# Graph network kernel: the rows of h and y turned by DMA transposes instead of TensorE transposes

## The reference

```python
def _layer(x, rows, cols, vals, W, b):            # first network, layers 0 and 1
    neigh = segment_sum(vals[:, None] * x[cols], rows)   # mean over neighbours
    return relu(concatenate([x, neigh], axis=1) @ W.T + b)
h = _layer(x, src, dst, 1/deg, W0, b0); h = _layer(h, ..., W1, b1)
y = layernorm(x + h)
z = y @ W_self + segment_sum(top32(y @ W_neigh)[src], dst) / deg_dst
out = layernorm(y + z)
```

## Time and profile before

| | |
|---|---|
| time, 3 runs | 677.92 us median (676.73 to 679.54) |
| span of the profiled execution | 680.0 us |
| TensorE busy | 650.4 us (96% of the span) |
| VectorE busy | 496.9 us (73%) |
| ScalarE busy | 338.8 us (50%) |
| GpSimd busy | 108.6 us (16%) |
| DMA queue of SyncE | 72.30 MB, 35.8% of 16 engines' time |

### The profile page before, as it was taken

The page is one execution under the profiler, slowest core; times in us unless marked ns, Lnnn a source line. Parts: engine busy times, 40 slices in busy tenths (PEclk is TensorE's granted clock), DMA queues, the critical chain, the costliest instruction groups (busy, mean ns, idle before and its releaser), DMA issues.

```text
span 680.0 us, 11272 instructions
## 1 busy us (share of the span) xinstructions
PE 650.4 (96%) x3982; PEld 337.4 (50%) x3983; DVE 496.9 (73%) x1274; ACT 338.8 (50%) x654; POOL 108.6 (16%) x187
## 2 busy tenths in 40 slices
PE   8788899999988999999999999999999999999996
PEld 3466566676534444444444444444444444444442
DVE  8898969999768788787882587878878855643333
ACT  3768779999768576767673233333333320000000
POOL 3001122222111001010110323222232210000000
PEclk9898979999999899999999999999999999999999
DMA  8643635555521111111112556565656423310000
GB/s 205 116 130 108 214 120 167 171 167 167 158 67 46 31 37 40 33 44 31 46 32 69 158 159 186 153 190 152 180 163 178 137 80 115 116 31 24 25 28 23
DMA packets 39543, 73.09 MB, mean 107 GB/s; under 512 B 3120, under 2 KB 32207, under 8 KB 39481
## 3 DMA queue, kind: packets, MB, share of 16 engines
q1 hardware_dynamic: 39481, 72.30, 35.8%
HBM read 38.91 MB, written 33.38 MB: 106 GB/s over the span
## 4 chain that ended last, share of the span: by engine, by line
PE 81%; DVE 10%; ACT 3%; DMA 2%; issue 2%; SPq 0%; POOL 0%; DVEq 0%; POOLq 0%; ACTq 0%
PE pair L1557 34%; PE bank L1681 10%; PE pair L1681 10%; PE bank L1481 6%; PE bank L1455 5%; PE bank L1447 4%; PE pair L1455 4%; PE pair L1367 4%; DVE hots L637 2%; PE bank L1461 1%; DVE tree L820 1%; DMA own_in<-own_dram 1%; DMA wparts_dram<-w_parts 1%; PE pair L1346 1%; PE bank L1467 1%
## 5 line engine op out<-in xcount | busy, mean ns | idle before, releaser
L1557 PE MATMUL pair<-xs,ct 125*128 125x512 f16 x625 | 143.7, 380 | 0.0
L1557 PE MATMUL pair<-a,ct 125*128 125x512 f16 x625 | 142.8, 379 | 0.0
L637 DVE TENSOR_TENSOR hots<-iota,jobs 125x1792 f16<-125x1792 f16 (+1 forms) x100 | 103.1, 1064 | 5.0 <-PE pair L1367 4.4
L1557 PEld LDWEIGHTS pair<-a,ct 125*128 125x128 f16 x625 | 61.1, 99 | 68.1
L1557 PEld LDWEIGHTS pair<-xs,ct 125*128 125x128 f16 x625 | 60.9, 100 | 67.6 <-issue 1.4
L1068 ACT ACTIVATE slab<-pair 125x875 f16<-125x875 f32 (+1 forms) x100 | 83.3, 854 | 13.2 <-PE pair L1367 8.6
L1226 ACT ACTIVATE a<-ct 125x1000 f16<-125x1000 f16 (+1 forms) x75 | 80.2, 1069 | 8.2 <-DMA c_dram<-slab 7.3
L1681 PE MATMUL bank<-xs,ct 125*128 125x512 f16 (+1 forms) x325 | 71.5, 379 | 0.0
L1681 PE MATMUL pair<-xs,ct 125*128 125x512 f16 x300 | 66.4, 379 | 0.0
L529 POOL TENSOR_TENSOR own_in<-own_in,bias_sb 125x256 f32<-125x256 f32 x50 | 38.2, 765 | 168.3 <-DMA own_in<-own_dram 168.2
L1301 ACT ACTIVATE sd<-mv,epsb 125x1 f32<-125x1 f32 x25 | 7.4, 294 | 113.9 <-DVE mv L1004 113.9
(11 more groups left out here) (205 smaller groups left out, 829.7 us busy)
## 6 DMA issues: line engine op xcount, KB each, us to landing
c_dram<-slab SPq DMA_DIRECT2D x25, 683.6 KB
ct<-c_dram SPq DMA_DIRECT2D x25, 683.6 KB
own_in<-own_dram SPq DMA_DIRECT2D x50, 125.0 KB
own_dram<-own SPq DMA_DIRECT2D x25, 125.0 KB
own_dram<-own_st SPq DMA_DIRECT2D x25, 125.0 KB
x_in<-in_x_dram SPq DMA_DIRECT2D x25, 125.0 KB
z_dram<-z_st SPq DMA_DIRECT2D x25, 125.0 KB
a<-z_dram SPq DMA_DIRECT2D x5, 625.0 KB
```

The costliest lines, as they stand in the source:

```text
L637: v.tensor_tensor(hots[k][:, :, :, :].rearrange("p w g (a d) -> p (w g) a d", d=2), iota, job, ALU.is_equal).then_inc(win_hot, 1)
L1557: ins = mm(agg[k % 3][0:lhs.shape[1], :], lhs, parts[l][:, t, :], start=t == 0, stop=t == NT - 1, skip_group_check=True)
```

## The change

The 50 turns leave TensorE, and the 50 copies from PSUM leave ScalarE. In their place SyncE issues 50 DMA transposes (`turn(i)`), which read `part` (now 128 partitions high, its last rows cleared by GpSimd) and write `tr_sb` at once, four 128 x 128 blocks each. `turn` waits for the complete `part` and for the product that last read this `tr_sb`; `product` and the next writer of `part` wait for the semaphore that the DMA raises at its end (`turned`). In layer 1, `load_c(T - 1)` moves to the place right behind `turn`, ahead of `load_own`, `load_x` and `store_z`. A few products of the first tiles stand at other blocks.

```diff
-        part = [lay(f"part{i}", [P, 2 * F], F16) for i in range(2)]
+        part = [lay(f"part{i}", [128, 2 * F], F16) for i in range(2)]
...
+            def turn(i):
+
+                sp.wait_ge(y_ready if i >= NT else lo_ready, i % NT + 1)
+                if i > 1:
+                    sp.wait_ge(mm_done, i - 1)
+                sp.dma_start_transpose(tr_sb[i % 2][:, :, :], part[i % 2][:, :]).then_inc(turned[i % 2], 16)
...
             for T in range(NT):
                 if T + 2 < NT:
                     load_own(0, T + 2)
+                turn(T)
                 if T:
                     store_own1(T - 1)
...
             for T in range(NT):
+                if T:
+                    turn(NT + T - 1)
+                    sp.wait_ge(agg_done, NT + T + 1)
+                    load_c(T - 1)
                 if T + 2 < NT:
                     load_own(1, T + 2)
                     load_x(T + 2)
                 if T > 1:
                     store_z(T - 2)
-                if T:
-                    sp.wait_ge(agg_done, NT + T + 1)
-                    load_c(T - 1)
+            turn(2 * NT - 1)
...
-            for t in tr_sb:
-                nc.gpsimd.memset(t[:, :, P:128], 0.0).then_inc(tr_zeroed, 1)
+            pool.wait_ge(a0_split, NT + 2)
+            for i, t in enumerate(part):
+                nc.gpsimd.memset(t[96:128, :], 0.0).then_inc(part_zeroed, 1)
+                pool.wait_ge(part_zeroed, i + 1)
...
-            def tr_out(i):
-                act.wait_ge(tp_done, i + 1)
-                if i > 1:
-                    act.wait_ge(mm_done, i - 1)
-                a.activation(tr_sb[i % 2][:, :, 0:P], tp[i % 2], ACT.Copy).then_inc(tp_copied, 1)
...
             def product(i):
 
-                pe.wait_ge(tp_copied, i + 1)
+                pe.wait_ge(turned[i % 2], 16 * (i // 2 + 1))
...
-            turn_h(0)
             aggregate(0, 2, 9, 20)
-            product(0)
             degrees(2)
             aggregate(0, 2, 20, NT)
-            turn_h(1)
-            aggregate(0, 3, 0, 9)
+            product(0)
+            aggregate(0, 3, 0, 8)
             product(1)
-            aggregate(0, 3, 9, 17)
+            aggregate(0, 3, 8, 17)
...
-            for T in range(5, NT):
-                aggregate(0, T, 0, 17)
-                turn_h(T - 1)
-                aggregate(0, T, 17, NT)
+            for T in range(4, NT):
+                aggregate(0, T, 0, NT)
                 if T + 1 < NT:
                     degrees(T + 1)
                 product(T - 1)
...
-            aggregate(1, 0, 0, 11)
-            turn_h(NT - 1)
-            aggregate(1, 0, 11, 17)
+            aggregate(1, 0, 0, 20)
             product(NT - 1)
-            aggregate(1, 0, 17, NT - 2)
-            aggregate(1, 1, 0, 12)
+            aggregate(1, 0, 20, NT - 2)
+            aggregate(1, 1, 0, 14)
...
             for T in range(2, NT):
-                aggregate(1, T, 0, 12)
-                turn_y(T - 2)
-                aggregate(1, T, 12, NT)
+                aggregate(1, T, 0, NT)
                 product(NT + T - 2)
```

More of the change, by code:

```diff
@@ L257, in gnn @@
         xp = bank[7][:, 0:2 * P].rearrange("p (c n) -> p c n", c=2)
-        tp = [bank[i][:, 0:4 * P].rearrange("p (c n) -> p c n", c=4) for i in (5, 6, 7)]
         agg, dense = bank[0:3], bank[3:5]
@@ L543, in y_low @@
                 pool.wait_ge(y_high, T + 1)
-                out = part[T % 2]
+                out = part[(NT + T) % 2][0:P, :]
                 nc.gpsimd.tensor_tensor(out[:, F:2 * F], t2[(NT + T) % 2][:, :], out[:, 0:F], ALU.subtract).then_inc(y_ready, 1)
@@ L918, in _ @@
                 dve.wait_ge(hi_ready, T + 1)
-                v.scalar_tensor_tensor(part[T % 2][:, F:2 * F], t2[T % 2][:, :], 0.0, part[T % 2][:, 0:F],
+                v.scalar_tensor_tensor(part[T % 2][0:P, F:2 * F], t2[T % 2][:, :], 0.0, part[T % 2][0:P, 0:F],
                                        ALU.max, ALU.subtract).then_inc(lo_ready, 1)
@@ L1210, in h_high @@
                 part_free(T)
-                a.activation(part[T % 2][:, 0:F], t2[T % 2][:, :], ACT.Relu).then_inc(hi_ready, 1)
+                a.activation(part[T % 2][0:P, 0:F], t2[T % 2][:, :], ACT.Relu).then_inc(hi_ready, 1)
             def own1_out(T):
@@ L1240, in _ @@
                     degree(T + 1, 0)
[L1241 to L1244 removed]
                 if T == 0:
+                    act.wait_ge(part_zeroed, 2)
                     h_high(0)
@@ L1276, in y_high_part @@
                 part_free(NT + T)
-                a.activation(part[T % 2][:, 0:F], t2[(NT + T) % 2][:, :], ACT.Copy).then_inc(y_high, 1)
+                a.activation(part[(NT + T) % 2][0:P, 0:F], t2[(NT + T) % 2][:, :], ACT.Copy).then_inc(y_high, 1)
             def sp_high_part(T):
@@ L1457, in in_parts @@
                 return last
-            def turn(out, parts, done):
-                for c in range(4):
-                    last = mm(out[:, c, :], parts[:, c * 128:(c + 1) * 128], ident16[:, 0:P], start=True, stop=True)
-                last.then_inc(done, 1)
             def own_transposes(t, rows_):
@@ L1560, in aggregate @@
                     ins.then_inc(agg_done, 1)
-            def turn_h(T):
-                pe.wait_ge(lo_ready, T + 1)
-                if T > 1:
-                    pe.wait_ge(tp_copied, T - 1)
-                turn(tp[T % 2], part[T % 2], tp_done)
-            def turn_y(T):
-                pe.wait_ge(y_ready, T + 1)
-                pe.wait_ge(tp_copied, NT + T - 1)
-                turn(tp[(NT + T) % 2], part[T % 2], tp_done)
             def product(i):
-                pe.wait_ge(tp_copied, i + 1)
+                pe.wait_ge(turned[i % 2], 16 * (i // 2 + 1))
                 if 1 < i < NT + 2:
@@ L1626, in _ @@
                 layer_start()
-            turn_h(0)
             aggregate(0, 2, 9, 20)
-            product(0)
             degrees(2)
             aggregate(0, 2, 20, NT)
-            turn_h(1)
-            aggregate(0, 3, 0, 9)
+            product(0)
+            aggregate(0, 3, 0, 8)
             product(1)
-            aggregate(0, 3, 9, 17)
+            aggregate(0, 3, 8, 17)
             degrees(3)
             aggregate(0, 3, 17, NT)
-            turn_h(2)
-            aggregate(0, 4, 0, 9)
             product(2)
             degrees(4)
-            aggregate(0, 4, 9, 20)
-            turn_h(3)
-            aggregate(0, 4, 20, NT)
-            degrees(5)
-            product(3)
-            for T in range(5, NT):
-                aggregate(0, T, 0, 17)
-                turn_h(T - 1)
-                aggregate(0, T, 17, NT)
+            for T in range(4, NT):
+                aggregate(0, T, 0, NT)
                 if T + 1 < NT:
@@ L1657, in _ @@
             pe.wait_ge(a1_lo, NT - 2)
[L1658 to L1660 removed]
+            aggregate(1, 0, 0, 20)
             product(NT - 1)
[L1662 to L1663 removed]
+            aggregate(1, 0, 20, NT - 2)
+            aggregate(1, 1, 0, 14)
             pe.wait_ge(a1_lo, NT)
             aggregate(1, 0, NT - 2, NT)
[L1666 removed]
+            aggregate(1, 1, 14, NT)
             for T in range(2, NT):
[L1668 to L1670 removed]
+                aggregate(1, T, 0, NT)
                 product(NT + T - 2)
```

18 lines of the change are left out of this document (3 added, 15 removed).

## The result

The changed kernel takes 673.25 us (median of 6 runs, 672.78 to 675.38) beside 677.6 us for the kernel before on the same chip (6 runs, 676.47 to 679.54): a ratio of 0.993, interval 0.9905 to 0.9955. It is faster, by 4.35 us, where the prediction said 10 (667.9 us, with a range of 665.0 to 677.5). Executions over 1.5% above the fastest of their kernel count in the medians and spreads given here but not in the ratios, which makes a difference for the two kernels with counts or transposes of layer 1 on a queue of their own beside narrow transfers.

The account below looks back on a forecast made before the run. TensorE was taken as the bound, busy for 96% of the span. Gains of 1.9, 4.2 and 5.2 us less 1.2 lost between the layers made 10.1 us: 667.9 us on the median, range 665.0 to 677.5.

Parts of the forecast that it names:

- Removed turns, 0.22 us each, on the path: Both layers: each TensorE turn costs 0.22 us of a tile; 50 are 10.8 to 11.0 us if all counted.
- L of 3.33 us in layer 0: Time from complete `part` until `product` may start, read from a plain load in layer 0; ends 0.6 and 7.77 us.
- The cover of 4.65 us: Layer 0: time from complete `part` to its product's turn on TensorE, hiding the transpose's 3.33 us with 1.3 to spare.
- First tiles, -2.1 with turn 5: Start of layer 0: one long TensorE wait becomes three short ones; 1.9 us gained up to tile 5, 2.1 with turn 5.
- the 1.7 us of clock: First tiles: 1.7 us gained because TensorE's clock stays up without the 2.45 us wait for tile 5's degree counts.
- Between the layers, +1.2: Layer 0 to 1: product 25 waits for own rows, then its transpose; 21.0 instead of 19.8 us, so 1.2 lost.
- Layer 1, -5.2: Rest of layer 1 and start of the last sum: turns 26 to 49 removed, 24 x 0.216 = 5.2 us gained.
- The cover is 6.8 us, near the upper end of L: Layer 1: 6.8 us from the end of `y_low` to its product, two aggregates later, available to hide the transpose.
- It costs nothing unless it takes over 10 us: Layer 1: `load_c` moved forward puts 763 KB ahead of own and x rows wanted more than 10 us after issue.
- The third rival: VectorE's loop at 6.9 us or layer 1 transposes queued behind counts over 6.8 us: within 0.5%, 675 to 679; chance 0.05.
- VectorE at 6.64 us a tile at most: Layer 0: VectorE needs at most 6.64 us a tile, under the new 6.78, so it keeps up.

Follow-up runs that it names:

- the control: The kernel before, without DMA transposes, with its 125-row transfers (own, x, z, bias) cut into 112 and 13 rows: 677.44 us, ratio 0.9978.
- the spread transfers: The changed kernel with all its 125-row transfers (own rows of both layers, bias, x, z) cut into 112 and 13 rows: 666.97 us, ratio 0.9827.

## Why the prediction was right in its parts and wrong in its size

- **Removed turns, 0.22 us each, on the path:** right. 18 of them are 3.95 us between products 5 and 23, and 22 are 4.83 in layer 1 once nothing waits.
- **L of 3.33 us in layer 0, between 0.6 and 7.77:** right in kind, a little high. `part` of tile 2 is complete at 206.44 and product 2 starts at 209.16, 2.72 us; the landing there is 2.4 to 3.6. The cover of 4.65 us was never used up, so no wait, as said. Of the two rules of the Trainium skill weighed in the prediction, that of "Advanced Engine Details and Errata" (X-Bar Transpose), as fast as a plain DMA, agrees. By that of "VectorE: DVE Perf Modes" (The three transpose paths), taken for four blocks one after the other, it would be an estimated 5.2 us, and the trace has 2.4 to 3.6 for all four where the engines are free. (At 5.2 us the prediction's own terms give a gain of about 2 us and not of 3: 1.0 lost in layer 0, 5.2 gained in layer 1, 3.1 lost between the layers, 1 gained in the first tiles.)
- **First tiles, -2.1 with turn 5:** -2.25 against the one execution, -0.85 against the control's, so the number is partly luck: the 1.7 us of clock in the sum came from one execution. Three short waits and no slow clock came, but not the three that were worked out: none ahead of product 1 (1.4 said), 1.03 ahead of product 2 (1.4), 0.26 ahead of the counts of tile 4 (none said), 0.76 ahead of those of tile 5 (0.6). And the wait ahead of the second half of tile 2's blocks is 2.33 us where it was 1.26 before; the profile names no cause for either.
- **Between the layers, +1.2:** +1.45, and here errors cancelled. The own rows were issued 1.5 us later than before (1.0 said) and took 0.5 longer (none said), and from the end of `y_low` at 371.66 to product 25 it was 2.5 us (3.33 said). The cause was named (own rows, then the transpose); that the own rows are slow because they run on five engines was not seen.
- **Layer 1, -5.2: the step that failed.** "The cover is 6.8 us, near the upper end of L" was right, but the sum then took the latency as hidden. It was not: landing 7.3 us in the median and up to 8.2, from issue to product up to 8.3, waits of 0.3 to 0.8 ahead of some products and shorter ones ahead of others, 5.4 us in all beside the spread transfers (152.73 against 147.28), and with them the whole gain gone (+0.61 from product 25 to 47, +0.25 to the end). L was measured in layer 0, where the queue was empty, and carried to layer 1, where it is full; the row of the same load under traffic, 7.77 us, was kept as a bound and not as layer 1's price. And on moving `load_c` forward, "It costs nothing unless it takes over 10 us" asked only who wants the own and x rows, not where their 125-row transfers leave the next transpose. The third rival had the mechanism in part (transposes of layer 1 behind other transfers for over 6.8 us), but named the counts alone and gave it 5 in 100.
- **VectorE at 6.64 us a tile at most:** right. It still waits for TensorE in layer 0, up to 0.3 us a time (0.15 said).

## What to carry to other kernels

A latency is a property of the queue it was read in: before a wait is moved onto a DMA, add up what the DMA engines do in one period of that stage, engine by engine, and compare with the cover there. Look at the row counts of the small transfers: 125 rows kept two thirds of the DMA engines out, and 27 us lay between cutting them at row 112 and at row 124. The packets showed it most directly: behind transfers of 125 rows a transpose stopped with five sixteenths of its packets to go, behind transfers of 124 rows with four sixteenths. Where TensorE is the bound, a DMA transpose does replace its turns at their full price, 10.5 us here, once its transfer is as short as the cover; the plain changed kernel got less than half of it, and the version with own rows cut (666.56 us) is the fastest that ran, level with the full cut.

## What the runs showed of the hardware that was not expected

- A 128 KB DMA transpose, fp16, SBUF to SBUF, lands 2.4 us after its issue at the quickest, and its issue takes SyncE 1.19 us, against 0.25 for a plain load.
- While transfers of 125 rows run, the DMA engines move 113 GB/s at a share of 0.33; of 124 rows, 93 GB/s at 0.27; the counts, in 112 and 13 rows, 300 GB/s at 0.94.
- A transpose of 512 packets queued behind 125-row transfers passes 350 of them, stops for up to 3.0 us and passes the other 162; behind 124-row ones it is 382 and 130; behind those of 112 and 13 rows it hardly ever stops.
- One small change of the load on the engines goes a long way: the same transposes landed at a median of 2.5 us (spread), 3.3 (one of three spread), 7.3 (none) and 9.1 (none, counts ahead).
- A second queue for the transposes made them land later (median 6.6 instead of 2.5 with spread transfers). With the counts moved there and the narrow transfers kept, the median fell from 7.3 to 5.4, but single transposes took up to 12.1.
- A wait of 2.6 us of TensorE was followed by full clock in one execution, and one of 2.45 us by half clock in another.
